# Four-layer sequence model on one core: row-wise dot products in the second layer, 16-bit code transposes in the first, and a re-ordered start of the attention scores

## The reference

```python
# layer 0: every linear layer quantises its input row by row to whole numbers -127..127
def _act_quant(x):
    scale = 127.0 / jnp.clip(jnp.max(jnp.abs(x), axis=-1, keepdims=True), 1e-05)
    return jnp.clip(jnp.round(x * scale), -128, 127) / scale
# i, f, g = bitlinear(mx, wi|wf|wg); h = scan(silu(i)*(1-f), sigmoid(f)); x += gate*bitlinear(rmsnorm(h)*silu(g), wo)
# x += gate*bitlinear(silu(gate_half)*up_half, wm2), both halves from bitlinear(mlp_in, wm1), 256 -> 2 x 1024 -> 256
# layer 1
z = rmsnorm(x, norm_in_w) @ pre_w.T
folded = mean of z at t, t+1, t+2, t+3          # clamped at the end
gfold = folded * gate
target = style @ style_w.T                      # one row per batch
cos = jnp.sum(l2norm(gfold) * l2norm(target), axis=-1, keepdims=True)
scale = cfg * (1.0 + cos) * 0.5
y = concat([x, gfold + scale * (target - gfold)]) @ merge_w.T + merge_b
x = gelu(rmsnorm(y) @ ffn_w1.T + b1) @ ffn_w2.T + b2 + x
# layer 2: adaptive norm, attention with 16 heads of 16 and rotary embedding, softmax, MLP of 1024
# layer 3: a diagonal complex state space scan, MLP of 1024
```

## Time and profile before

| | |
|---|---|
| time, median of 3 runs | 1990.77 us (1985.62 to 1993.22) |
| profiled execution, its own time | 1985.53 us |
| its span, first to last instruction | 1983.7 us |
| TensorE, VectorE, ScalarE, GpSimd busy | 88%, 69%, 56%, 31% |
| mean granted TensorE clock | 0.938 of 2.4 GHz |
| `layers01` | about 88 to 887 us of the span |

### The profile page before, as it was taken

One profiled execution on the slowest core, in us unless ns is written; L12 is line 12 of the kernel. 1 busy time (PEld: TensorE's weight loads), 2 busy tenths in 40 slices (PEclk: granted clock), 3 DMA queues, 4 the chain that ended last, 5 costly groups with the idle time before them and its releaser, 6 DMA issues.

```text
span 1983.7 us, 25674 instructions
## 1 busy us (share of the span) xinstructions
PE 1747.9 (88%) x8444; PEld 1046.9 (53%) x8463; DVE 1359.0 (69%) x2873; ACT 1106.3 (56%) x2117; POOL 615.3 (31%) x874
## 2 busy tenths in 40 slices
PE   1367677989999999878989999999999998999998
PEld 1145455667667657543344444454545444666666
DVE  5755888888887765567867686877686734566650
ACT  6634667868867753314675757566666664322221
POOL 0145556756754633620000001010101012334342
PEclk9756788999999999988999999999999999999999
DMA  9440000000000002303030303030303005000000
GB/s 373 123 158 1 10 19 20 12 9 19 14 1 14 20 4 65 65 17 64 5 67 5 67 5 67 5 67 4 67 4 67 4 4 149 3 11 22 11 22 21
DMA packets 94422, 83.57 MB, mean 42 GB/s; under 512 B 9881, under 2 KB 87842, under 8 KB 94034
## 3 DMA queue, kind: packets, MB, share of 16 engines
q1 hardware_dynamic: 94192, 81.91, 15.1%
...
q10 hardware_dynamic: 98, 0.03, 0.0%
...
## 4 chain that ended last, share of the span: by engine, by line
PE 40%; DVE 8%; ACT 6%; issue 1%; POOL 0%; POOLq 0%; DVEq 0%; ACTq 0%
PE k_psum L88 13%; PE k_psum L2518 6%; PE k_psum L2044 5%; PE k_psum L2105 5%; PE k_psum L2158 5%; PE k_psum L2035 4%; PE k_psum L94 3%; DVE l_small L2194 2%; ACT l_prob L1983 1%; ACT L1983 1%; ACT L1999 1%; ACT l_gu L1999 1%; DVE l_xn L2267 1%; DVE l_small L2181 1%; DVE l_xn L2269 1%
## 5 line engine op out<-in xcount | busy, mean ns | idle before, releaser
L2194 DVE TENSOR_REDUCE l_small<-k_psum 128x1 f32<-128x512 f32 x512 | 329.7, 685 | 134.9 <-PE k_psum L2158 131.5
L1983 ACT ACTIVATE l_prob<-k_psum 128x512 f32<-128x512 f32 x512 | 286.4, 596 | 184.5 <-PE k_psum L2035 181.3
L1971 POOL TENSOR_TENSOR k_x_res<-k_x_res,k_arena_a 128x256 f32<-128x256 f32 x32 | 23.2, 726 | 418.5 <-DVE k_arena_a L2238 418.5
L2044 PE MATMUL k_psum<-l_prob,l_v 128*32 128x512 f32 x1024 | 138.1, 612 | 0.2
L2105 PE MATMUL k_psum<-k_arena_a,l_gu 128*128 128x256 f32 x512 | 135.6, 394 | 0.7 <-ACT l_gu L1999 0.7
L88 PE MATMUL k_psum<-l_turned_over,k_arena_a 128*128 128x512 f32 x256 | 120.8, 596 | 4.2 <-ACT l_gu L1999 4.2
L88 PE MATMUL k_psum<-k_arena_b,l_w_f 128*128 128x512 f32 x256 | 122.0, 604 | 0.0
L1461 PE MATMUL k_psum<-l_w_f,k_arena_b 128*128 128x256 f32 x512 | 120.4, 380 | 0.2 <-ACT k_arena_b L1274 0.2
L88 PE MATMUL k_psum<-l_hT,k_arena_b 128*128 128x512 f32 x256 | 114.3, 593 | 0.0
L2518 PE MATMUL k_psum<-k_arena_b,l_gu 128*128 128x256 f32 x512 | 113.0, 379 | 0.0
L2105 PEld LDWEIGHTS k_psum<-k_arena_a,l_gu 128*128 128x128 f32 x512 | 98.1, 198 | 19.7 <-issue 2.2
...
## 6 DMA issues: line engine op xcount, KB each, us to landing
...
```

Source lines behind the costliest of these rows:

```text
L1983: act.activation(prob[:, s % 2, j, :], psum[:, 2 + n % 2, :], ACT.Exp, scale=float(HD) ** -0.5).then_inc(exp_ready.sem, 1)
L2044: last = pe.matmul(psum[j * BLOCK:(j + 1) * BLOCK, 4, :], v[e % 2][:, kt, at:at + BLOCK], prob[:, n % 2, j, :], start=(kt == 0), stop=(kt ...
L2194: dve.tensor_reduce(mx[:, n % T, n // T:n // T + 1], psum[:, n % 2, :], AX.X, ALU.max).then_inc(max_ready.sem, 1)
```

## The change

1. **Codes in 16-bit halves.** ScalarE now adds `ROUND + MIDDLE`, MIDDLE = 0x4380. The low 16 bits of the 32-bit word are then 0x4380 plus the code, a valid bf16 pattern. TensorE turns over only the low halves (`low`, every second bf16 element of the f32 tile), against the high halves of the identity (`identh`), into a bf16 output; six turns fit one bank (`halves`). VectorE reads the bank as uint16 (`codes`) and subtracts 0x4380. The wait of `xq` for `sg_ready` is gone.
2. **Dot products as two rows.** `dots` puts two columns (style vector and zero, then zero and one) in as the stationary operand and streams 512 tokens of `g` and of `gsq`: 4 f32 products of 512 columns into `psum[0:2, 3, :]`. ScalarE copies the 2 x 512 sums to SBUF (new stage `dots` in `ACT_TURN`), TensorE turns them over in 4 small turns (new stage `dotsT`, behind `o` 1), and `gg`, moved behind `stats` 1 and `x3` 3, reads them.
3. **Start of the attention.** Until score 48 of batch 0, bank 4 is a third score bank. The scores hang three at a time from `f2` 5 on and are through at `f2` 4 of the last batch. `ones` of batch 0 becomes one ScalarE exponential with scale 0 behind the last `gelu` of layer 1; `ones` of batch 1 becomes eight memsets of 3 x 1024. `ln1` and `xn` of attention batch 1 hang on `x3` 0 and `x3` 1 of the last batch.
4. Several setup semaphores are merged, three small memsets are added at GpSimd's start.

```diff
-    ("fi", 2, 1), ("silu", 0, 0), ("fi", 3, 1), ("gsq", 1, -1), ("silu", 1, 0), ("silu", 2, 0), ("ssqo", 0, 1), ("ssqh", 0, 0),
+    ("fi", 2, 1), ("silu", 0, 0), ("fi", 3, 1), ("gsq", 1, -1), ("silu", 1, 0), ("dots", 0, -1), ("silu", 2, 0), ("ssqo", 0, 1), ("ssqh", 0, 0),
...
-    ("mods", 0, 1), ("f2", 6, -3), ("gate", 1, 0), ("f2", 7, -3), ("dots", 0, -1), ("gate", 2, 0), ("up", 1, 0), ("o", 0, 1), ("o", 1, 1),
+    ("mods", 0, 1), ("f2", 6, -3), ("gate", 1, 0), ("f2", 7, -3), ("dots", 0, -1), ("gate", 2, 0), ("up", 1, 0), ("o", 0, 1), ("o", 1, 1), ("dotsT", 0, -1),
...
-    ("scan", 0, -1), ("x3", 2, -5), ("gg", 0, -3), ("stats", 1, 2), ("x3", 3, -5), ("h", 1, -2), ("xw", 3, 0), ("s", 0, -3), ("rinv", 0, -3),
+    ("scan", 0, -1), ("x3", 2, -5), ("stats", 1, 2), ("x3", 3, -5), ("gg", 0, -3), ("h", 1, -2), ("xw", 3, 0), ("s", 0, -3), ("rinv", 0, -3),
...
-    ("s5p", 4, B - 1): (("ones", 0, 0),),
...
+    ("gelu", 7, B - 1): (("ones", 0, 0),)}
...
-    ("f2", 5, B - 2): (("s", 2, 0), ("s", 3, 0)),
+    ("f2", 5, B - 2): (("s", 2, 0), ("s", 3, 0), ("s", 4, 0)),
...
-    ("f2", 7, B - 1): (("s", 46, 0), ("s", 47, 0))}
+    ("f2", 4, B - 1): (("s", 47, 0),)}
...
-    ("x3", 2, B - 1): (("s", 43, 0), ("s", 44, 0), ("s", 45, 0), ("ln1", 0, 1)),
-    ("x3", 3, B - 1): (("s", 46, 0), ("s", 47, 0), ("npart", 2, 0), ("xn", 0, 1))}
+    ("x3", 0, B - 1): (*(("s", n, 0) for n in range(38, 41)), ("nkeep", 1, 0), *(("s", n, 0) for n in range(41, 44)), ("ln1", 0, 1)),
+    ("x3", 1, B - 1): (*(("s", n, 0) for n in range(44, 47)), ("xn", 0, 1), ("s", 47, 0), ("npart", 2, 0))}
...
+        def low(a, cols):
+            return a.bitcast(BF16).rearrange("p (n a) -> p n a", a=2)[:, cols, 0]
+        identh = ident[:].bitcast(BF16).rearrange("p (n a) -> p n a", a=2)[:, :, 1]
+        def halves(a):
+            return psum[:, a, :].bitcast(BF16)
+        def codes(a):
+            return psum[:, a, :].bitcast(U16)
...
-                            pe.wait_ge(sg_ready.sem, sg_ready.at(e, t))
...
-                            last = turn(nc, two_banks(0)[:, tok(j)], xw[:, t, j // KD, tok(j % KD)], ident[:])
+                            last = turn(nc, halves(0)[:, tok(j)], low(xw[:, t, j // KD, :], tok(j % KD)), identh[:])
...
-                        V.tensor_scalar(qT[:, t % 2, :, :].rearrange("p a n -> p (a n)"), two_banks(0)[:, 0:3 * D], ROUND, None,
+                        V.tensor_scalar(qT[:, t % 2, :, :].rearrange("p a n -> p (a n)"), codes(0)[:, 0:3 * D], float(MIDDLE), None,
...
+                        mm(nc, psum[0:2, 3, :], [(style_pair[:, k, e, :], g[:, k, :]) for k in range(KD)] + [(pair, gsq[:, k, 0:L]) for k in range(KD)]).then_inc(summed.sem, 1)
+                    elif stage == "dotsT":
+                        pe.wait_ge(sums_ready.sem, sums_ready.at(e, 1))
                         for i in range(T):
-                            mm(nc, psum[:, 3, i:i + 1], [(g[:, k, tok(i)], styleT[:, k, e:e + 1]) for k in range(KD)])
-                        for i in range(T):
-                            last = mm(nc, psum[:, 3, T + i:T + i + 1], [(gsq[:, k, tok(i)], one[:]) for k in range(KD)])
+                            last = turn(nc, psum[:, 3, 2 * i:2 * i + 2], sums[:, tok(i)], ident[0:2, 0:2])
...
+    def banks_of(e, n):
+        return (0, 1, 4) if e == 0 and n < 48 else (0, 1)
...
-                if e:
-                    pool_chain.link(nc.gpsimd.memset(v[1][:], 1.0))
-                nc.gpsimd.memset(kT[e][SROWS:SROWS + MROWS, :, :], 1.0).then_inc(ones_ready, 1)
+                pool_chain.link(nc.gpsimd.memset(v[1][:], 1.0))
+                for h in range(0, HEADS, 2):
+                    nc.gpsimd.memset(kT[1][SROWS:SROWS + MROWS, h:h + 2, :], 1.0).then_inc(ones_ready, 1)
...
+            if stage == "ones":
+                act.activation(kT[0][SROWS:SROWS + MROWS, :, :].rearrange("p h n -> p (h n)"), ident[SROWS:SROWS + MROWS, 0:1].to_broadcast([MROWS, HEADS * L]),
+                               ACT.Exp, scale=0.0).then_inc(ones_ready, 1)
```

More of the change, by code:

```diff
@@ L17 @@
 BF16 = mybir.dt.bfloat16
+U16 = mybir.dt.uint16
 B, L, D = 8, 512, 256
@@ L760, in layers01 @@
         b_merge, b_f2, gateT, style = sb("b_merge", [P, D]), sb("b_f2", [P, D]), sb("gateT", [P, KD, L]), sb("style", [P, D])
-        small = Small(sb("small", [P, 400]))
-        half, one = small(B), small(1)
+        small = Small(sb("small", [P, 416]))
+        half, pair = small(B), small(2)
+        one = pair[:, 1:2]
         bn, mv, var, rstd, away = small(T, 6), small(T, 2), small(T), small(T), small(T)
@@ L968, in _ @@
                 gp.memset(half[:], -0.5).then_inc(half_ready, 1)
-                gp.memset(one[:], 1.0).then_inc(half_ready, 1)
+                gp.memset(one, 1.0).then_inc(half_ready, 1)
+                gp.memset(pair[:, 0:1], 0.0).then_inc(half_ready, 1)
+                gp.memset(style_pair[:, :, :, 1], 0.0).then_inc(half_ready, 1)
                 gp.memset(ones, 1.0).then_inc(half_ready, 1)
-                pool.wait_ge(half_ready, 3)
+                pool.wait_ge(half_ready, 5)
                 for stage, t, e in steps(POOL_TURN):
@@ L1255, in _ @@
                         ac.activation(gsq[:, t, 0:L], g[:, t, :], ACT.Square).then_inc(gsq_ready.sem, 1)
+                    elif stage == "dots":
+                        act.wait_ge(summed.sem, summed.at(e, 1))
+                        ac.activation(sums, psum[0:2, 3, :], ACT.Copy).then_inc(sums_ready.sem, 1)
                     elif stage == "ssq4":
@@ L1321, in _ @@
                         for k in range(KD):
-                            last = turn(nc, psum[:, t % 2, tok(k)], xo[:, t, tok(k)], ident[:])
+                            last = turn(nc, halves(t % 2)[:, tok(k)], low(xo[:, t, :], tok(k)), identh[:])
                         last.then_inc(xo_turned.sem, 1)
@@ L1337, in _ @@
                             for k in range(KD):
-                                last = turn(nc, psum[:, 4 + t, tok(KD * i + k)], mx2[:, 2 * t + i, tok(k)], ident[:])
+                                last = turn(nc, halves(4 + t)[:, tok(KD * i + k)], low(mx2[:, 2 * t + i, :], tok(k)), identh[:])
                         last.then_inc(turned2.sem, 1)
@@ L1355, in _ @@
                         for k in range(T):
-                            last = turn(nc, psum[:, 4 + (3 * i + c) % 2, tok(k)], h[:, i, tok(c * T + k)], ident[:])
+                            last = turn(nc, halves(4 + (3 * i + c) % 2)[:, tok(k)], low(h[:, i, :], tok(c * T + k)), identh[:])
                         last.then_inc(h_turned.sem, 1)
```

127 lines of the change are left out of this document (63 added, 64 removed).

## The result

The changed kernel takes 1962.89 us (median of 4 runs, 1956.41 to 1964.26) against 1991.99 us of the kernel before beside it: 0.9854 of its time, interval 0.9823 to 0.9885. It is faster, by 29 us; the forecast was 63 us. The profiled execution has a span of 1961.6 us, 22.1 us under that of before. Single executions of one kernel lie up to some 18 us apart, and the profiled one need not be near the median; the table further on gives both.

A forecast was written before the change was run, and what follows sets the result against it. Early a chain through all engines was taken to bound the kernel, in the middle TensorE, then the handoff. Early 21, middle 27 and handoff 14 made 62 us: 1923.5 own time, 1928 us forecast, range 1905 to 1965.

The forecast's parts named there:

- rival 1: TensorE's turns gain nothing because the 4-byte step keeps 105 ns; the middle's 21 us are lost: 1949 us, chance 0.13.
- rival 4: The clock falls behind dots nonetheless, since only two columns are weights: 1943 us, chance 0.09.
- rival 2: VectorE or the new ring (dots, ScalarE, dotsT, gg, h) becomes the bound; half is saved in the middle: 1945 us, chance 0.13.
- Turns: TensorE's 576 turns: 0.049 us less each in bf16, 28 us over all, 21 of it in the middle.
- rival 5: A bf16 turn is bound by loading its 128 x 128 weights, 0.080 us; the middle loses 10 us: 1938 us, chance 0.08.
- rival 6: Turning every second element takes more than an f32 turn, so the kernel is slower: 2016 us, chance 0.04.
- Copies: VectorE's copies on 16-bit input get shorter, 40 us of VectorE; 3 us of time counted, in the early stretch.
- Rival 3: VectorE's 16-bit reads run at the f32 pace; early chain and ring lose: 1938 us, chance 0.07.
- Dots: Full clock behind the dot products gains 12 us in the middle, 3.5 early and 1.7 in the handoff.
- The new wait: VectorE's wait for dotsT before gg in the middle: 0.7 us a round, 4 us over six rounds.
- The wait for `sg_ready`: Removing TensorE's wait between tiles in the early stretch: nine transitions at 1.6 us, 14 us, range 8 to 20.
- Handoff: From 775 to 887 us: memset gone beside npart, third score bank, earlier ln1 and xn; 15 us, less 1.

The follow-up runs named there:

- e1: Changed kernel with the old 32 one-column dot products and gg in its old place; 0.9812 of the time of before, 1952.1 us.
- e2: Changed kernel with its codes put back to f32 turns over two banks, with the wait for sg_ready; 0.9924 of the time of before, 1974.2 us.
- e8: Changed kernel with GpSimd's 128 x 1024 multiplication hw 0 moved behind sgn 2 and rms; 0.9808 of the time of before, 1947.5 us.
- e10: Changed kernel with hw 0 moved later on GpSimd and the old 32-record dot products; 0.9775 of the time of before, 1943.8 us.
- e15: Changed kernel with xq's wait for sg_ready put back, 16-bit codes kept; 0.9869 of the time of before, 1959.1 us.
- e3: Changed kernel with two score banks, the GpSimd memset and the late ln1 and xn put back; 0.9962 of the time of before, 1980.1 us.

## Why the prediction was wrong

The direction was right and the time is inside the stated range (1905 to 1965), near its upper end. But 29 us came of 63, and the likeliest case's own range (1912 to 1942) does not hold it. That the wide range does is luck: it reaches up to 1965 for rivals 1 and 4, and neither came.

**The step that failed** is in the first part: "In the middle (357 to 775 us, six rounds of some 70 us) TensorE does, and only its own work, its clock and its waits count." TensorE was busy 69.5 of 72 us, which hid that the other engines came round at almost the same pace. Its work shrank by 3.5 us of turns a round, and the rounds did not: the time went into its waits for `h` and `xn`. Against the 27 us summed for the middle stands a loss of 4.0; even with `hw` 0 moved in both kernels the gain is 1.2. Taken apart, the codes (21 forecast) gave the middle 9.3 us before the rows went in (before to e1), and the rows (12 less 4, so 8 forecast) cost it 13.3 (e1 to the changed kernel). Which chain of the other engines sets the round stays open. I had deducted 2 us "for work that will meet another engine". This is rival 2, with its place rightly named but priced at half the gain instead of all of it. I put "its 57 of 72 us against" it: the mean share hid a stretch of 24 us almost without a gap, behind `gg`. Two sums of the prediction are wrong besides: half of the 27 us is 13.5, so rival 2 stood at 1942 and not 1945, and 6 and 10 us under 1928 is 1912, not the 1905 of the range.

**Turns**: 0.049 us each forecast, 0.052 measured; 576 of them, some 30 us of TensorE, are really gone. With the shorter copies and the missing wait for `sg_ready` they were worth 1.5 us of the middle as changed, 7.2 with `hw` 0 moved, and 6.6 early (e2). Rivals 1, 5 and 6 are out.

**Copies**: 404, 532, 277 ns forecast; 418, 549, 283 measured, and VectorE is busy 1320.0 us instead of 1359.0. Rival 3 is out.

**Dots**: the clock behind them is full, as forecast, so rival 4 is out. The new wait was the mis-sized term: 0.7 us a round against (15.2 - 4.6)/6 = 1.8 from e1 to the changed kernel, and in five of six rounds the clock fell behind one of these waits, which gave back what the full clock behind `dots` had gained: read in steps of 2 us, the clock below full cost 13.6 us in the middle, after 15.3 before. Even where it was gained in full (e8 against e10) it bought no time. I had counted only how late `gg` is, not what VectorE does behind it: TensorE reaches `up` 3 sooner, `h` 2 does not come sooner (11.3 us after `dots` starts, 10.9 before). I also misread one of the five stretches of half clock that I summed to 24 us as lying behind `dots`. In the kernel before, the clock stayed full for 12 us from the start of the third `dots`, and fell behind a wait of 2.71 us for `h`, which is what the change then brought to five of the six rounds:

```profile
417.60:421.50 3.90, 3.82 (x34) 3.69 (x35) 1.06 (x4) 0.00 (x0) 0.00 (x0) 1.00 0.00 0
430.00:433.40 3.40, 2.63 (x5) 1.25 (x6) 3.37 (x6) 2.83 (x9) 1.44 (x3) 0.50 0.00 0
```

```profile
428.59 0.59 PE L88 MATMUL k_psum<-k_t_wm,l_qT 128*128 128x512 bf16 x2 [2.71 <-DVE k_arena_a L1601]
```

**The wait for `sg_ready`**: 14 us forecast, nothing measured (e15). The tiles of batch 0 came 5.42 us apart; now it is 3.58, 3.56 and 4.00 us between the four starts:

```profile
118.69 1.46 PE L91 MATMUL k_psum<-k_t_ifg,l_qT 128*128 128x256 bf16 x6 [2.80 <-DVE l_qT L1538]
...
122.27 1.46 PE L91 MATMUL k_psum<-k_t_ifg,l_qT 128*128 128x256 bf16 x6 [1.47 <-DVE l_qT L1538]
...
125.83 1.46 PE L91 MATMUL k_psum<-k_t_ifg,l_qT 128*128 128x256 bf16 x6 [1.47 <-DVE l_qT L1538]
...
129.83 1.46 PE L91 MATMUL k_psum<-k_t_ifg,l_qT 128*128 128x256 bf16 x6 [1.90 <-DVE l_qT L1538]
...
248.54 1.11 PE L97 MATMUL k_psum<-k_ident,l_xn 128*128 128x128 f32 x4 [6.63 <-ACT l_xn L1252]
```

But what was taken away came back elsewhere. In the projections of batch 0 and 1 TensorE's waits for `qT` grew from 10.2 to 14.3 us, while those for the third activation (line 1187, 1175 before) fell only from 10.1 to 5.4, and at the first `xn` it waits 6.63 us, where it was 2.08 before:

```profile
255.74 1.11 PE L94 MATMUL k_psum<-k_ident,l_xn 128*128 128x128 f32 x4 [2.08 <-ACT l_xn L1240]
```

A removed wait is worth no more than the slack of what comes next in the chain, and I had summed nine of them without looking at what came next.

**Handoff**: 15 us forecast, 18.6 measured, 20.2 by e3 (in its slowest execution). `npart` lost its 6.7 us and the waits for maxima (12.4 us) fell to 1.0 us in 820 to 870. `ones` on ScalarE took 7.02 us and a table load in its idle time.
